# Selective scan: the fourth time chunk of du x B through a diagonal matrix on TensorE

## The reference, cut to what matters

```
def step(h, inp):
    d_t, u_t, B_t, C_t = inp
    dA = jnp.exp(d_t[..., None] * A)
    dBu = (d_t * u_t)[..., None] * B_t[:, None, :]
    h = dA * h + dBu
    y = jnp.einsum('bdn,bn->bd', h, C_t)
    return (h, y)
...
return jnp.swapaxes(ys, 0, 1) + u * Dp
```

## Time and profile before

| | |
|---|---|
| median of three runs | 2864.61 us |
| profiled execution | 2869.83 us, span 2868.0 us |
| both scans in the span | about 134 to 781 us and 882 to 1526 us |
| mean granted TensorE clock | 0.937 |

### The profile page before, as it was taken

The page is one execution under the profiler, slowest core; times in us unless marked ns, Lnnn a source line. Parts: engine busy times, 40 slices in busy tenths (PEclk is TensorE's granted clock), DMA queues, the critical chain, the costliest instruction groups (busy, mean ns, idle before and its releaser), DMA issues. The chain is left out here.

```text
span 2868.0 us, 38576 instructions
## 1 busy us (share of the span) xinstructions
PE 2351.8 (82%) x12386; PEld 1187.3 (41%) x12387; DVE 1956.9 (68%) x1797; ACT 1803.4 (63%) x2811; POOL 1312.1 (46%) x493
## 2 busy tenths in 40 slices
PE   7688888888886888888888767778879679978899
PEld 2344444444334444444443423223322445546444
DVE  7699999999758999999994475933751322216530
ACT  5799999999658999999993334045127311112441
POOL 2099998999705999999992111000000120020000
PEclk9799999999998999999999688889979799989999
DMA  2420001000114100100000120011001510020000
GB/s 95 111 49 27 26 29 38 30 26 26 50 43 119 30 26 26 45 26 26 26 22 17 39 82 31 1 31 30 1 9 42 224 41 22 22 87 1 10 1 29
DMA packets 61704, 115.63 MB, mean 40 GB/s; under 512 B 13587, under 2 KB 21907, under 8 KB 60576
## 3 DMA queue, kind: packets, MB, share of 16 engines
q1 hardware_dynamic: 52992, 103.20, 11.4%
q0 software_dynamic: 8608, 11.05, 1.3%
HBM read 86.39 MB, written 27.53 MB: 40 GB/s over the span
## 5 line engine op out<-in xcount | busy, mean ns | idle before, releaser
L1175 POOL TENSOR_TENSOR hs<-hs,c_bc 128x2048 f32<-128x2048 f32 x256 | 1166.6, 4557 | 64.5 <-DVE hs L1226 48.3
L1226 DVE TENSOR_TENSOR_SCAN hs<-decays,ps 128x512 f32<-128x512 f32 x512 | 611.0, 1216 | 26.2 <-PE ps L1253 8.1
L1226 DVE TENSOR_TENSOR_SCAN hs<-decays,carry,ps 128x512 f32<-128x512 f32 x512 | 621.1, 1269 | 9.1 <-PE ps L1253 7.7
L1261 PE MATMUL ps<-hs,sel 128*64 128x512 f32 x2048 | 500.1, 609 | 14.3 <-POOL hs L1175 13.9
L1253 PE MATMUL ps<-ident,dbu_even 128*128 128x128 f32 x2048 | 296.2, 284 | 92.4 <-DVE hs L1226 64.6
L1253 PE MATMUL ps<-ident,dbu_odd 128*128 128x128 f32 x2048 | 294.7, 283 | 92.1 <-DVE hs L1226 61.5
L1189 ACT ACTIVATE decays<-delta_far,A 128x512 f32<-128x512 f32 x512 | 355.6, 707 | 10.3 <-DVE hs L1226 10.1
L1189 ACT ACTIVATE decays<-delta_near,A 128x512 f32<-128x512 f32 x512 | 356.2, 707 | 3.3 <-DVE hs L1226 3.3
L1197 ACT ACTIVATE dbu_odd<-du_turned,b_turned 128x512 f32<-128x512 f32 x512 | 355.6, 706 | 0.0
L1197 ACT ACTIVATE dbu_even<-du_turned,b_turned 128x512 f32<-128x512 f32 x496 | 344.5, 706 | 0.0
L1253 PEld LDWEIGHTS ps<-ident,dbu_even 128*128 128x128 f32 x2048 | 220.5, 142 | 243.0 <-DVE hs L1226 189.2
(11 more groups left out here) (283 smaller groups left out, 2629.5 us busy)
## 6 DMA issues: line engine op xcount, KB each, us to landing
c_bc<-c_rows SPq DMA_DIRECT2D x256, 128.0 KB, 2.9
o_rows<-osb SPq DMA_DIRECT2D x32, 256.0 KB
u_rows<-u SPq DMA_DIRECT2D x4, 1024.0 KB, 4.3
d_rows<-delta SPq DMA_DIRECT2D x4, 1024.0 KB, 4.0
delta_near<-d_rows SPq DMA_DIRECT2D x4, 1024.0 KB, 10.1
hs<-u_rows SPq DMA_DIRECT2D x4, 1024.0 KB, 6.8
delta_far<-d_rows SPq DMA_DIRECT2D x4, 1024.0 KB, 12.8
w_down<-in_expert_proj SPq DMA_DIRECT2D x1, 4096.0 KB, 36.3
```

The costliest lines, as they stand in the source:

```text
L1175: pool.tensor_tensor(x, x, spread(c_bc[:, g, :], 4), ALU.mult).then_inc(weighed.sem, 1)
L1226: dve.tensor_tensor_scan(hs[:, quad % RING, n, :], decays[:, s % RING, :], ps[:, DBU + s % RING, :], carry[:, at(i * GB, g), blk] if q els ...
L1261: mm = pe.matmul(ps[lo:lo + DB, ACC + quad % 2 * 2 + j // 2, :], k.sel2[:, :], hs[:, quad % RING, j, :], start=False, stop=False, skip_gro ...
```

## The change

In each group the two products of the fourth time chunk (t = 3, n = 0 and 1) are no longer made by ScalarE as 128x512 slices. ScalarE writes instead two 128x128 diagonal matrices, the identity scaled per partition by B, into a new buffer `b_diag` with one pair for even and one for odd groups. In `turn`, the fourth transpose of each unit is replaced by two matmuls. Each takes the 128x64 block of `du_turned` as the stationary operand and a diagonal of 128x128 as the moving one. The first writes PSUM partitions 0 to 63, the second 64 to 127, 128 columns each. Number, order and semaphores of the ScalarE instructions stay. The same is done for the first group in `first_products`.

```diff
+        b_diag = k.sb("b_diag", [P, 2, PAIR, P], ctx=ctx)
...
                     for n in range(PAIR):
+                        if t == QT - 1:
+                            act.activation(b_diag[:, 0, n, :], k.ident[:], ACT.Copy, scale=b_t[:, t, n:n + 1])\
+                               .then_inc(prefilled.sem, 1)
+                            continue
                         act.activation(first_dbu[:, t, :, n, :], du_t[:, t, :].rearrange("p (b d) -> p b d", d=DB),
                                        ACT.Copy, scale=b_t[:, t, n:n + 1]).then_inc(prefilled.sem, 1)
...
         chunk = q * QT + t
+        if t == QT - 1:
+            return (b_diag[:, (g + 1) % 2, n, :], k.ident[:], b_t[:, chunk, at(i * (GB * PAIR), (g + 1) * PAIR + n)])
...
                 pe.wait_ge(scanned.sem, count(scanned, q, i, UNITS, s + 1))
-                for t in range(QT):
-                    mm = pe.transpose(ps[:, DBU + s % RING, t * P:(t + 1) * P],
-                                      room[g % 2][:, t, blk, :, :].rearrange("p n d -> p (n d)"), k.ident[:])
+                for t in range(QT - 1):
+                    pe.transpose(ps[:, DBU + s % RING, t * P:(t + 1) * P],
+                                 room[g % 2][:, t, blk, :, :].rearrange("p n d -> p (n d)"), k.ident[:])
+                t = QT - 1
+                for n in range(PAIR):
+                    mm = pe.matmul(ps[n * DB:(n + 1) * DB, DBU + s % RING, t * P:(t + 1) * P],
+                                   du_t[:, q * QT + t, blk * DB:(blk + 1) * DB], b_diag[:, g % 2, n, :],
+                                   start=True, stop=True)
                 mm.then_inc(turned.sem, 1)
```

More of the change, by code:

```diff
@@ L743, in mamba @@
             with ExitStack() as bctx:
-                mamba_batch(k, b, a, room, flat, w, w_out, vec, A, diag, bctx)
+                mamba_batch(k, b, a, room, b_diag, flat, w, w_out, vec, A, diag, bctx)
 def scan_weights(a, flat):
@@ L754, in scan_weights, with mamba_batch @@
     return (w_in, w_x, w_dt), [(w_in, a["w_in"]), (w_x, a["w_x"]), (w_dt, a["w_dt"])]
-def mamba_batch(k, b, a, room, flat, w, w_out, vec, A, diag, ctx):
+def mamba_batch(k, b, a, room, b_diag, flat, w, w_out, vec, A, diag, ctx):
     X = k.X
@@ L767, in mamba_batch @@
     with ExitStack() as c2:
-        scan_inputs(k, b, flat, xn, w, vec, A, diag, zs, du_t, b_t, near, room[0], c2)
+        scan_inputs(k, b, flat, xn, w, vec, A, diag, zs, du_t, b_t, near, room[0], b_diag, c2)
     reload = []
@@ L773, in mamba_batch @@
     with ExitStack() as c2:
-        scan(k, b, A, room, du_t, b_t, near, diag, zs, reload, c2)
+        scan(k, b, A, room, b_diag, du_t, b_t, near, diag, zs, reload, c2)
     tiles = []
@@ L781, in mamba_batch, with scan_inputs @@
     project(k, tiles)
-def scan_inputs(k, b, flat, xn, w, vec, A, diag, zs, du_t, b_t, near, first_dbu, ctx):
+def scan_inputs(k, b, flat, xn, w, vec, A, diag, zs, du_t, b_t, near, first_dbu, b_diag, ctx):
     nc, ps = k.nc, k.ps
@@ L1076, in spread_delta, with scan @@
         sp.dma_start(to[n * DB:(n + 1) * DB, :, :], rows[:, :, h * W:(h + 1) * W]).then_inc(here.sem, 16)
-def scan(k, b, A, room, du_t, b_t, near, diag, zs, reload, ctx):
+def scan(k, b, A, room, b_diag, du_t, b_t, near, diag, zs, reload, ctx):
     nc, ps = k.nc, k.ps
```

## The result

The changed kernel takes 2931.17 us (median of four runs, 2925.61 to 2938.10) against 2863.92 for the kernel before (four runs). The ratio is 1.0233, 95% interval 1.0216 to 1.0249: slower. The profiled execution took 2931.11 us, 61.3 more than the profiled one of before.

The account below looks back on a forecast made before the run. ScalarE was taken as the bound at 4.90 us a quad, TensorE as the next at 5.08; +57 us in steady stretches and +4 outside gave +61 on 2864.6, so 2925 us, range 2880 to 2975.

Parts of the forecast that it names:

- Part 1: ScalarE: two of 16 instructions per group shrink to 128x128, each step from 0.61 to 0.29 us; a quad needs 4.58.
- Part 2: TensorE in the steady scan: it becomes the bound at 5.08 us a quad against 4.85.
- The two halves side by side: TensorE: the pair's two half-width products overlap, streaming in 0.22 us, its four records within 0.45 us.
- the rival of a slower pair: TensorE: the pair's small loads come late, 0.05 to 0.15 us more a pair, 2975 to 3070 us; chance 0.10.
- The price of a passage: TensorE: each switch between 128-wide and 64-wide products costs about 0.15 us, eight per quad instead of two.
- The steady stretches: Two per batch entry, 61 quads each: +14.0 and +14.7 us, +28.7 per entry, +57 for two.
- the finer split: TensorE per quad: eight late loads of 0.09, eight first products longer by 0.05, no restart for sums; given as 5.06 us.
- the plain sum: TensorE per quad: transposes 1.31, pairs 0.87, sums 1.72, eight width switches 1.20, together 5.10 us.
- Part 3: Outside the steady stretches: start, middle, end and prefilled products of a batch entry, +1.8 us per entry, +4 for two.
- The start of an entry: First 20 us of a batch entry: longer turns ahead of the first `skip`, 0 to +6 us, taken as +3.
- The middle of the first entry: Middle of a batch entry: TensorE's wait for u hides nearly all that two quads gain in length, +0.7 us left.
- the passages are hidden: Rival: TensorE at or below 4.6 us a quad, halves at GpSimd's 4.77 and VectorE's 4.70, 2838 us; chance 0.08.

Follow-up runs that it names:

- ScalarE's part alone: Kernel before with ScalarE making two diagonals for two slices; four transposes a unit stay, the fourth repeating the third chunk, fourth chunk's values left out: 2825.46 us, ratio 0.9878.
- six-passage run: Changed kernel with only unit 0 of each quad issuing its 64-wide pair before its transposes, six width changes per quad instead of eight: 2849.46 us, ratio 0.9959.
- four-passage order: Changed kernel with units 0 and 2 of each quad issuing the 64-wide pair before the transposes, four width changes per quad instead of eight: 2826.96 us, ratio 0.9883.

## Why the prediction was right

**The bound before.** ScalarE's 4.90 us a quad, with GpSimd's 4.77 and VectorE's 4.70 behind: the run with ScalarE's part alone went just to these two, 4.76 in a first half as shown and 4.69 in a second.

**Part 1.** The short form was taken at 0.29 us a step. In the changed kernel a diagonal starts at 477.63 and the next decay at 477.92:

```profile
477.63 0.39 ACT L1204 ACTIVATE b_diag<-ident,b_turned 128x128 f32<-128x128 f32 x1
...
477.92 0.71 ACT L1196 ACTIVATE decays<-delta_far,A 128x512 f32<-128x512 f32 x1
```

**Part 2.** 5.08 us a quad was forecast, 5.10 measured. The two halves side by side hold: the four records of a pair span 0.44 us, as the earlier trace rows had suggested for 32 columns, so the rival of a slower pair had no ground. The price of a passage was 0.15 forecast and 0.148 measured. The steady stretches gained 15.5 and 16.1 us, the same in both batch entries, 63.2 in all, where +57 was forecast. What was low is the step from 5.10 to 5.08: I had mixed in the finer split, whose terms as written add up to 5.02 and not to 5.06, and the plain sum was the nearer one. By the difference of 0.02 us a quad the forecast lost 6 us. The price of a passage comes from the six-passage run. The Trainium skill, TensorEngine Tiling (Array Packing), Key Properties, states that changing the tiling mode drains TensorE. The trace of the changed kernel agrees: at seven of a quad's eight passages the load stands 0.17 us idle, and behind the sums the turns start about 0.1 us after their steps of 0.43 us have run out.

**Part 3.** Forecast +4, measured 61.3 - 63.2 = -2. The start of an entry, from the first turn to the turns of the fourth quad, takes 21.25 and 21.23 us in the two entries, against 20.40 and 20.00: +0.9 and +1.2 instead of +3, at a granted clock of 0.84 against 0.68 and 0.74. The middle of the first entry got 2.2 us shorter instead of 0.7 longer: 21.15 (465.94 to 487.09) against 23.38. There the granted clock stayed at 1.00, where it had been 0.85, and `skip` ran 3.70 us instead of the 6.67 of the earlier trace rows, though it waited for u as before:

```profile
481.59 3.70 PE L1250 MATMUL ps<-hs,diag_skip 128*128 128x512 f32 x8 [1.99 <-DMA hs<-u_rows]
```

In the second batch entry of the kernel before, its timeline has 3.70 us too:

```profile
1212.53 3.70 PE L1243 MATMUL ps<-hs,diag_skip 128*128 128x512 f32 x8 [2.31 <-DMA hs<-u_rows]
```

That entry compares like with like, both kernels at a granted clock of 1.00: its middle takes 21.18 us against 20.20, +1.0, near the +0.7 of the sum. So the 2.2 us gained in the first entry belong to the clock of this pair of executions and are not shown to be an effect of the change. From the last quad to the output projection the two entries got 2.1 and 0.7 us shorter, where 1.3 was forecast for each.

Part 2 was 6 us too low and Part 3 6 us too high. They cancel: +61 forecast, +61.3 in the profiled executions, +67 between the medians. That the total agrees to 0.3 us is luck; the pace of a quad and the price of a passage are not.

**The rivals.** That the passages are hidden is refuted by the runs with fewer of them. The bounds that it named, 4.77 and 4.70, were right; the four-passage order reached them by removing passages, 32 us below the kernel before where 27 had been expected.

## What to carry to other kernels

Count, on TensorE, the places where the width of the stationary tile changes, and price them like instructions: 0.15 us here, more than the one further step of 0.109 us that the change added to each unit. Products of one width belong together, also across units, since the order inside a unit is free as long as the last one signals. Relief of the bounding engine is worth only the distance to the next ones, here 4.85 to 4.79 and 4.84 to 4.68 us; the work handed over must fit below that.

## What the runs showed of the hardware that was not expected

TensorE's busy time is no measure of its reserve. In the four-passage kernel it is busy without a break in a second half, though one unit's transposes in each quad wait for a scan:

```profile
500.00:700.00 200.00, 200.00 (x1540) 113.93 (x1536) 200.00 (x172) 198.02 (x343) 194.89 (x44) 1.00 0.08 28
```

The recorded length of a short matmul (0.27 us) outlasts its step (0.109 us), so waits of 0.2 us vanish beneath the tails; the idle time of the weight loads still shows them. In the changed kernel the eight passages, 1.2 of 5.10 us a quad, count as busy in the same way. VectorE too is busy 200 of 200 us here. That it is the bound rests on more than that: the pace of 4.68 us is the 4.70 that its own scans need, and TensorE waits for it.
